# A two-layer cross-attention and FFN kernel: in layer 0, GpSimd's low parts and inverse deviation ahead of its probabilities, the second normalisation behind the maxima, and the down product's wait split by chunk

## The reference

```python
x = x + _L0_xattn_ref(_layernorm(x, axis=-1), ctx_768, L0_xattn_Wq, ...)
x = x + _L0_ffn_ref(_layernorm(x, axis=-1), L0_ffn_w_gate, L0_ffn_w_up, L0_ffn_w_down)
x = x + _L1_xattn_ref(_layernorm(x, axis=-1), ctx_768, L1_xattn_Wq, ...)
x = x + _L1_ffn_ref(_layernorm(x, axis=-1), L1_ffn_rhs)

# _xattn_ref
scores = jnp.einsum('bqhd,bkhd->bhqk', q, k) * scale
attn = jax.nn.softmax(scores, axis=-1)
out = jnp.einsum('bhqk,bkhd->bqhd', attn, v).reshape(B, Nq, h * dh)
return out @ Wo + bo

# _L0_ffn_ref
gate = jnp.einsum('bsd,hd->bsh', x, wg)      # hidden width 768
up = jnp.einsum('bsd,hd->bsh', x, wu)
h = jax.nn.silu(gate) * up
return jnp.einsum('bsh,dh->bsd', h, wd)
```

## Time and profile before

| | |
|---|---|
| time, median of 3 runs | 1758.61 us (1753.06 to 1759.71) |
| the profiled execution's own time | 1756.78 us |
| its span in the profile | 1754.7 us |
| TensorE busy (matmul) | 1566.0 us, 89% |
| VectorE busy | 1375.5 us, 78% |
| ScalarE busy | 1324.4 us, 75% |
| GpSimd busy | 1245.7 us, 71% |
| mean granted clock of TensorE | 0.968 of full speed |

### The profile page before, as it was taken

How to read it: one execution, slowest core, us unless ns; L and a number is a source line. 1 busy time by engine, 2 the same in 40 slices (tenths; PEclk the granted TensorE clock), 3 DMA queues, 4 the chain that set the end, 5 groups by cost and what they waited for, 6 DMA issues and landing times.

```text
span 1754.7 us, 75093 instructions
## 1 busy us (share of the span) xinstructions
PE 1566.0 (89%) x27410; PEld 1358.7 (77%) x27410; DVE 1375.5 (78%) x3522; ACT 1324.4 (75%) x5514; POOL 1245.7 (71%) x1966
## 2 busy tenths in 40 slices
PE   7999778898888888898888888889999999999995
PEld 4556568787888878888888787777888888888884
DVE  6777557777777777777777777678999999999996
ACT  6665767777777677777777776677888888888883
POOL 5110467777777777777777777567999999999984
PEclk9999989999999899999999999999999999999998
DMA  9997796866666676666766787767989989888995
GB/s 251 342 321 259 168 191 136 153 148 146 152 149 149 140 155 156 144 146 144 162 141 152 144 156 135 140 133 153 196 198 194 193 198 193 197 191 198 191 185 115
DMA packets 740023, 307.79 MB, mean 175 GB/s; under 512 B 629201, under 2 KB 725361, under 8 KB 737841
## 3 DMA queue, kind: packets, MB, share of 16 engines
q1 hardware_dynamic: 738049, 299.32, 77.1%
q0 software_dynamic: 1840, 6.82, 1.4%
HBM read 87.09 MB, written 65.54 MB: 87 GB/s over the span
## 4 chain that ended last, share of the span: by engine, by line
PE 36%; POOL 18%; DVE 18%; issue 10%; DMA 5%; SPq 2%; DVEq 0%; ACT 0%; POOLq 0%
PE psum L333 26%; POOL pr L1707 6%; PE psum L1274 5%; PE psum L1237 4%; POOL hT_l L1698 4%; POOL p L1720 4%; DMA x2T<-x 3%; POOL p L1712 3%; DVE nmax L1544 2%; DVE oT_l L362 2%; DVE x L373 2%; POOL rs L395 2%; SPq L1125 1%; DVE st L378 1%; DVE sg L1509 1%
## 5 line engine op out<-in xcount | busy, mean ns | idle before, releaser
L1421 ACT ACTIVATE ex<-psum,nmax 128x77 f32<-128x77 f32 x2048 | 635.7, 331 | 66.5 <-DVE nmax L1544 51.4
L1707 POOL TENSOR_TENSOR pr<-ex,rden 128x308 f32<-128x308 f32 x512 | 399.3, 780 | 186.1 <-DVE rden L1549 185.7
L1421 ACT ACTIVATION_READ_ACCUMULATOR ex<-psum,nmax 128x1 f32 x2048 | 435.7, 213 | 0.0
L1712 POOL TENSOR_TENSOR p<-pr,p 128x308 f16<-128x308 f32 x512 | 388.3, 758 | 40.8
L333 PE MATMUL psum<-xT,wq_h 128*64 128x256 f16 x4064 | 356.3, 277 | 0.9 <-DMA xT<-x 0.9
L1544 DVE TENSOR_REDUCE nmax<-psum 128x4 f32<-128x308 f32 x512 | 238.0, 465 | 68.8 <-PE psum L1237 68.5
L333 PE MATMUL psum<-xT,wq_l 128*64 128x256 f16 x2032 | 282.4, 274 | 0.0
L333 PE MATMUL psum<-wo_h,oT_h 128*64 128x256 f16 x1792 | 259.0, 284 | 14.1 <-DVE oT_l L362 13.7
L333 PE MATMUL psum<-wo_h,oT_l 128*64 128x256 f16 x1792 | 257.3, 282 | 0.0
L333 PE MATMUL psum<-wo_l,oT_h 128*64 128x256 f16 x1792 | 256.5, 281 | 0.0
L1720 POOL CAST p<-pr 128x308 f16<-128x308 f32 x509 | 227.4, 447 | 38.9 <-DMA pT<-p 6.2
(11 more groups left out here) (173 smaller groups left out, 3504.7 us busy)
## 6 DMA issues: line engine op xcount, KB each, us to landing
keys<-ks SPq DMA_DIRECT2D x16, 1232.0 KB, 7.7
kb<-keys SPq DMA_DIRECT2D x256, 77.0 KB, 2.7
vb<-vals SPq DMA_DIRECT2D x128, 154.0 KB
vals<-vs SPq DMA_DIRECT2D x64, 256.0 KB, 4.5
x_pair<-in_x_dram SPq DMA_DIRECT2D x32, 256.0 KB, 3.0
pT<-p SPq DMA_TRANSPOSE x512, 3.2
x_res<-in_x_dram SPq DMA_DIRECT2D x32, 256.0 KB, 3.1
mid_x<-y SPq DMA_DIRECT2D x32, 256.0 KB, 2.4
```

The source lines that it names most:

```text
L1421: last = act.activation(ex[i][:, t, b, :], SC[:, t, b * NK:(b + 1) * NK], ACT.Exp, bias=nmax[i][:, t, b:b + 1], accum_out=den[i][:, t, b:b ...
L1707: pool.tensor_tensor(pr[:, t, :, :], ex[i][:, t, :, :], r, ALU.mult).then_inc(s_p, 1)
L1712: pool.tensor_tensor(d[:, t, 1, :, 0:NK], pr[:, t, :, :], d[:, t, 0, :, 0:NK], ALU.subtract).then_inc(s_pl, 1)
```

## The change

In the bodies of layer 0:

- GpSimd makes the low part of chunk 2 and the inverse deviation of the second normalisation in unit 0, ahead of the probabilities of unit 0; that of chunk 3 at the start of unit 1, and that of chunk 5 in unit 1, ahead of the probabilities of unit 1. Before, each stood one place later.
- VectorE makes `x2` right behind the maxima of unit 1 instead of behind `qT_l`; and the low part of chunk 4 ahead of `oT_l` in unit 2 instead of behind it.
- ScalarE makes the high part of chunk 5 behind `oT_h` of unit 2 instead of ahead of it, and the high part of `x2` in unit 2, behind `qT_h`, instead of at the end of unit 1.
- SP issues the transpose of `x2` ahead of the two transposes of `pT` of unit 1.
- `down(0)` waits for the low parts of chunks 0 to 3 at its start, for chunk 4 ahead of chunk 4 and for chunk 5 ahead of chunk 5.

No instruction is added or taken away but for the semaphore waits.

```diff
@@ sync
+                        if u == 2 and lay[-2] == 0:
+                            turn_second_rows(h - 2)
                         if turning:
                             turn_probabilities(n + u - 1, (u - 1) % UNITS, 0)
...
                         if turning:
                             turn_probabilities(n + u - 1, (u - 1) % UNITS, 1)
-                        if u == 2 and lay[-2] == 0:
-                            turn_second_rows(h - 2)
@@ tensor
-                def down(t, o):
+                def down(t, o, b):
                     terms = [(c, hh) for c in range(HC) for hh in (hT_h, hT_l)]
                     for q, (c, hh) in enumerate(terms):
+                        if t == 0 and q == 0:
+                            pe.wait_ge(s_hlp, len(LOW_POOL) * b + LOW_POOL.index(3) + 1)
+                            pe.wait_ge(s_hld, len(LOW_DVE) * b + LOW_DVE.index(1) + 1)
+                        if t == 0 and (c, q % 2) == (4, 0):
+                            pe.wait_ge(s_hld, len(LOW_DVE) * (b + 1))
+                        if t == 0 and (c, q % 2) == (5, 0):
+                            pe.wait_ge(s_hlp, len(LOW_POOL) * (b + 1))
...
-                            pe.wait_ge(s_hlp, len(LOW_POOL) * (h - 2))
-                            pe.wait_ge(s_hld, len(LOW_DVE) * (h - 2))
-                            down(0, bank("down", 0))
+                            down(0, bank("down", 0), h - 3)
@@ scalar
-                        if u == 2 and lay[-3] == 0:
-                            high_hidden(5, h - 3)
...
+                        if u == 2 and lay[-3] == 0:
+                            high_hidden(5, h - 3)
                         if lay[(u + 1) // UNITS] is not None:
...
                             high(act, qT_h[(u + 1) % 2][:, :, :], RG[(u + 1) % 2], Q_DOWN).then_inc(s_qh, 1)
+                        if u == 2 and lay[-2] == 0:
+                            act.wait_ge(s_x2, QT * (h - 1))
+                            after(act, s_x2d, 16 * (h - 2))
+                            high(act, x216[:, :, 0, :], x2[:, :, :]).then_inc(s_x216h, 1)
...
-                        if u == 1 and lay[-2] == 0:
-                            act.wait_ge(s_x2, QT * (h - 1))
-                            after(act, s_x2d, 16 * (h - 2))
-                            high(act, x216[:, :, 0, :], x2[:, :, :]).then_inc(s_x216h, 1)
@@ vector
+                        if u == 2 and lay[-3] == 0:
+                            low_hidden(4, h - 3)
                         if lay[-1] is not None:
                             dve.wait_ge(s_oh, n + u - 3)
                             low(dve, oT_l[u % 2][:, :, :], weighed(like, u), oT_h[u % 2][:, :, :]).then_inc(s_ol, 1)
-                        if u == 2 and lay[-3] == 0:
-                            low_hidden(4, h - 3)
...
+                        if u == 1 and lay[-2] == 0:
+                            normalise_rows(dve, 1, x2, x1[1 - odd], mv2, rs2, h - 1, s_x2)
                         if u == 1 and lay[-3] == 0:
                             sigmoid_gate(4, h - 3)
                             hidden(4, h - 3)
...
-                        if u == 1 and lay[-2] == 0:
-                            normalise_rows(dve, 1, x2, x1[1 - odd], mv2, rs2, h - 1, s_x2)
@@ gpsimd
                         if u == 1 and lay[-3] == 0:
-                            low_hidden(2, h - 3)
-                        if u == 2 and lay[-3] == 0:
-                            low_hidden(5, h - 3)
+                            low_hidden(3, h - 3)
...
                         if u == 1 and lay[-3] == 0:
-                            low_hidden(3, h - 3)
+                            low_hidden(5, h - 3)
+                        if u == 0 and lay[-3] == 0:
+                            low_hidden(2, h - 3)
+                        if u == 0 and (lay[-2] == 0 or lay[-3] == 0):
+                            inverse(pool, 1, ve2, rs2, h - 1)
...
-                        if u == 0 and (lay[-2] == 0 or lay[-3] == 0):
-                            inverse(pool, 1, ve2, rs2, h - 1)
```

More of the change, by code:

```diff
@@ L1370, in body @@
                         if u == 2 and lay[-3] == 0:
-                            down(1, bank("down", 1))
+                            down(1, bank("down", 1), h - 3)
                         if u == 2 and lay[-2] == 1:
```

## The result

The changed kernel takes 1645.96 us (median of 4 runs, 1643.63 to 1651.91), the kernel before, timed beside it, 1759.16 us (4 runs): a ratio of 0.936, with a 95% interval of 0.931 to 0.941. The forecast was 1650 us. The profiled execution took 1644.1 us; its span is 1642.1 us, 112.6 less than before.

The account below looks back on a forecast made before the run. It took layer 0's bodies as bound by TensorE's work plus waits for `hT_l` and `x2T`, caused by order; 26 bodies x (28.94 - 25.3) = 95 us, plus 12, makes 107 less than 1756.8: 1650 us, range 1605 to 1698.

Parts of the forecast that it names:

- The mechanism: Ahead of `down(0)`: reordering lets GpSimd's low part 5 start at 452.0 instead of 454.92, so TensorE's 3.03 us wait goes whole.
- the 2 us asked for: Sign of being right: the low part of chunk 5 comes within 2 us of the start of unit 2's scores.
- The next limit: GpSimd's chain through `xn` to unit 3's exponentials becomes late next: a body of about 25.3 us, against 24.2 for TensorE alone.
- the engines crowd: Rival: `pr` stretched in every set of unit 1 and `x2T` landing late, 26.0 us a body, 1670 us; chance 0.18, shared with the clock.
- `x2` (1.17 for both halves) only changes place: VectorE, unit 1: moving `x2` leaves its time at 1.17 us, while `hf` of chunks 4 and 5 lose 1.65 us of waits.
- The stretch of GpSimd's own: GpSimd's chain, beside VectorE's two-input instructions: contention over SBUF would cost it up to 0.4 us more.
- The prediction's sum: 26 bodies x (28.94 - 25.3) = 95 us, plus 12 us for the last five bodies: 107 us less, 1650 us.
- The last five bodies: Bodies with a down product after the 26: 9 us of `hT_l` waits and some for `x2T`, taken as 12 us.
- counted the wait as gone: TensorE's 1.53 us wait for `x2T` ahead of the first gate product: landing at 457.6 to 459.3, wanted at 458.3.
- On the path they cost little: TensorE's lowered clock in layer 0's FFN: some 35 us of pace lost, but the followed body at full clock takes 28.72 against 28.94.
- Its bound of 35 us: If the clock kept falling as often without the `x2T` wait covering it, up to 35 us would show.
- spare cover: Splitting `down(0)`'s wait by chunk: the 3.03 us wait goes whole even without it.

Follow-up runs that it names:

- e7_inv_first: The changed kernel with GpSimd's inverse deviation and shift for `xn` ahead of its last set of probabilities of unit 1: 1628.17 us, ratio 0.927.
- e11_after_dve_act_old: The changed kernel with VectorE's and ScalarE's order of before; GpSimd's order, SyncE's move and the split wait stay: 1634.65 us, ratio 0.930.
- e8_inv_first_x2T_first: The changed kernel with GpSimd's inverse deviation and shift for `xn` earlier, and the transpose of `x2` also ahead of the keys on SyncE: 1625.40 us, ratio 0.925.
- e1_split_only: The kernel before with only the wait of `down(0)` split by chunk: 1796.93 us, ratio 1.021.
- e3_pool_only: The kernel before with only GpSimd's list in the new order: 1769.56 us, ratio 1.006.
- e6_x2T_only: The kernel before with only the transpose of `x2` moved ahead of the `pT` transposes of unit 1 on SyncE: 1707.77 us, ratio 0.972.
- e10_before_filled: The kernel before plus 26 matmuls a body, results overwritten, ahead of `down(0)` in its wait for `hT_l`: 1777.53 us, ratio 1.010.
- e4_after_x2T_late: The changed kernel with only SyncE's move undone, the transpose of `x2` back behind the `pT` transposes of unit 1: 1796.53 us, ratio 1.023.

## Why the prediction was right, and where it wasn't

*The mechanism held.* The low part 5, the bound of the kernel before, came in time; `down(0)` waits for nothing. `hf` lost its waits, and low part 5 starts 1.2 us behind the scores of unit 2 (426.64), within the 2 us asked for.

*The next limit held, nearly to the tenth.* The prediction had `xn` 458.3 - 440.14 = 18.2 us into the body, the exponentials of unit 3 at 21.2 and the next scores 4.23 later. In the body shown they are at 434.29 - 415.83 = 18.46, 437.35 - 415.83 = 21.52, and 441.58 - 437.35 = 4.23 later. The run `e7_inv_first` bears the chain out. The prediction's own links end at 461.35 + 4.23 = 465.58, a body of 25.44 us; the 25.3 of the forecast takes off 0.14 ("or somewhat before") for which it has no row. The wait ahead of unit 0's scores is 0.57 us, where about 1 was expected.

*Mis-sized: the body.* 25.3 us was forecast, 26.05 measured: 75 us in 26 bodies instead of 95. That is outside the 25.0 to 25.7 of the forecast and is the 26.0 of the rival "the engines crowd", though not by its terms: `pr` stayed at 0.69 us (428.61) and the landing at 3.4. Of the 0.75 us, 0.3 to 0.45 lie in the chain, as above. The rest is mainly the kind of body of 26.25 us, in which `x2` takes 1.77 us (449.41) instead of the 1.17 that the prediction carried over from the earlier trace rows; `qT_l` stands behind it and TensorE waits 0.54 us for it, then 0.94 us for `oT_l`. The step that failed is "`x2` (1.17 for both halves) only changes place". `e11_after_dve_act_old` puts that part of the change at +0.4 us a body. The stretch of GpSimd's own that I had allowed for showed as a cast of 0.79 instead of 0.44 us (429.36), beside VectorE's low part of `x2`. By the Trainium skill, "SBUF — State Buffer", section "Who interferes with whom", such a VectorE instruction with two SBUF inputs and a GpSimd one that reads SBUF keep each other out; the cast's 0.35 us agrees with the 0.4 that was allowed. That VectorE's own rows stretch too, the prediction did not count: `ve` of 430.95 takes 0.72 us and ends at 431.67, as GpSimd's `pr` of 430.94 ends at 431.65. The same section names the tensor-scalar form, which `x2` and `ve` have, as one that can take the shared ports; the ends of `ve`, counted in the last section, agree, but no run here isolates it.

*Mis-sized the other way: what lies around the bodies.* The start, up to the first `down(0)`, became 282.65 - 270.49 = 12.2 us shorter, where nothing was counted. Some 3.3 us of it were there ahead of the first changed instruction. The rest are waits of the same two kinds, in the body ahead of the first `down(0)`: before, TensorE waited 3.89 us for `x2T` (to 258.31) and ran at a granted clock of 0.50 from 258.3 to 263.5, in the open; after, it waits 0.24 us at the same place, at a clock of 1.00; and the first wait for `hT_l`, 2.95 us, is gone. The prediction's sum began only with the first `down(0)` started. The last five bodies, from the 27th `down(0)` to the 32nd, gave 22.5 us instead of 12, and the rest 2.9. So 75.1 + 12.2 + 22.5 + 2.9 = 112.7 us against 107: the total is closer than its terms, since two errors cancel. That the time came within 4 us of 1650 is luck: with the 26.05 us a body and nothing else changed, the prediction's sum would have given 1670.

*Wrong in weight: `x2T`.* The prediction counted the wait as gone, worth 1.5 us a body, and named as a sign of being wrong that it is waited for in most bodies. It is, in 17 of the 26, mostly for 0.3 to 0.9 us: by that sign this step failed, though it costs little. The cause is the issue of two keys, 1.23 us, ahead of it on SyncE: in `e8_inv_first_x2T_first`, where it goes first, no such wait is left from 400 to 900 us. But without SyncE's move the same change would have been 2.3% slower than before. It was two conditions on one path, not the sum of two gains: GpSimd's move alone gives nothing (+0.6%), SyncE's alone 2.8%, both with the split wait 7.0% (`e11_after_dve_act_old`), and with VectorE's and ScalarE's moves, which cost a little, 6.4%.

*The clock.* "On the path they cost little" was right for the bodies of the kernel before, and by luck of their place: `e1_split_only`, `e3_pool_only`, `e6_x2T_only` and `e10_before_filled` each have half clock where nothing covers it, and pay for it in the bodies that have it. With both waits shortened it did not fall once from 283 to 1000 us, as the prediction expected. Its bound of 35 us came from a mean of 0.96; in `e4_after_x2T_late`, at 0.89, filling the wait, and so keeping the clock, is worth 73.

*The split of the wait* was spare cover, as said: 6 us or nothing.

## What to carry to other kernels

When two waits stand behind one another on the engine that is the bound, removing the first is worth only what the second leaves: look where the second one's transfer is issued, and move both. Price a wait of TensorE's together with the rows behind it: where the granted clock shows 0.50 over the next 5 us, the wait of 3.7 us costs 6, unless another wait follows that swallows the rest. And a mean clock doesn't tell whether it costs: look at the stretched rows, and whether a wait stands behind them that shrinks by as much. Check also that a total that comes out as forecast does so by its terms.

## What the runs showed of the hardware

TensorE's half clock behind a wait for `x2T`, counted by body between 283 and 1000 us (a gate or up row of 8 matmuls over 0.7 us within 6 us of the wait's end): behind waits of 3.7 us and more 24 of 24 (`e4_after_x2T_late`), of mostly 2.7 us 20 of 24 (`e1_split_only`), of mostly 2.8 us 15 of 25 (`e3_pool_only`), of mostly 1.64 us 15 of 24 (`e10_before_filled`). In the kernel before none of 12, eight of them of 1.5 to 2.1 us; in after none of 18, the longest 1.35 us, and none behind the one of 3.32 us that ended at 279.10, just ahead of that stretch. Behind the wait for `hT_l` of 3.0 us it fell in 17 of 24 bodies before and in 8 of 26 in `e6_x2T_only`. So the length of the wait alone does not decide it. That waits of 1.6 us were followed by it I hadn't expected, nor that 30 idle matmuls in a wait of 3.7 us make a kernel 72.6 us faster.

VectorE's `ve`, on 256 numbers, takes 0.17 to 0.72 us by what GpSimd does beside it. In the kernel before, from 300 to 940 us, no GpSimd instruction was running as it began, and it took 0.17 us in 67 of 67. In after one was running in 73 of 74, and in all 73 `ve` ended 0.02 to 0.03 us behind the end of that instruction. `x2` takes 1.07 to 1.77 us. That GpSimd holds VectorE up is what these ends say; no run takes GpSimd's instruction away to test it.
